# Experts phase: the down router's logits from column tiles of stationary padded weights, with an ACT copy and a folding matmul

## Chip, cores and metric

The kernel runs on one core of one Trainium2 chip. The metric is the device time of one execution in microseconds (us), the median of several runs.

## What is computed

Four blocks are applied to `x` of 16 sequences x 256 tokens x 128 features, each with a residual and a layer norm around it: a state-space block, a mixture of experts, a second state-space block, and six transformer layers. The change is in the mixture of experts, cut here to what matters (`E`=8 experts, `K`=2 kept, `H`=128, `I`=512):

```python
def _moe_linear(x, router_w, expert_w):
    logits = x @ router_w.T
    vals, idx = jax.lax.top_k(logits, K)
    probs = jax.nn.softmax(vals, axis=-1)
    onehot = jax.nn.one_hot(idx, n_exp, dtype=x.dtype)
    combine = jnp.einsum('tk,tke->te', probs, onehot)
    out = jnp.zeros((x.shape[0], expert_w.shape[1]), x.dtype)
    for e in range(n_exp):
        out = out + combine[:, e:e + 1] * (x @ expert_w[e].T)
    return out
xt = x.reshape(b * s, h)
g = _moe_linear(xt, router_gate, w_gate)
u = _moe_linear(xt, router_up, w_up)
inter = jax.nn.silu(g) * u
d = _moe_linear(inter, router_down, w_down)
```

All data is float32. Each float32 matmul of the program stands in the profile as two MATMUL instructions with a weight load each, so counts of rows are twice those in the code.

## The kernel before

`program` runs four phases. `ssm_phase` loads everything that comes later while it computes; `ExpertWeights.fetch` issues the expert weights on SP's queue there. `moe_phase` goes over the 16 sequences in 17 passes; there is no scheduler, each engine runs its own program text and the engines meet at semaphores (`Steps` counts them by name). Pass n does the gate and up routing of sequence n (`R`) and the experts of sequence n-1 (`M`).

In TensorE's program (`run` in the block `tensor`) a pass is, in order: the gate experts into PSUM `pg` (`m_experts(0, ..)`, line 748, with the router logits `r_lg`, line 719, after the first quarter), the up experts into `pu` (`m_experts(1, ..)`), the transposed routing weights (`r_ct`, 728), the transpose of the next sequence (`r_xt`, 709), the down router `m_ld` (line 761), and the down experts of the two token halves into `pdown[0]` = `pg` and `pdown[1]` = `pd` (`m_down(0)`, `m_down(1)`, line 772). `it` is the activated input of the down experts, 4 chunks of 128 features x 256 tokens. In `m_ld` the 128x128 pieces of `it` are stationary and 8 columns of `rd` are streamed.

What turns one pass into the next: ACT copies the transposed routing weights out (`cT`, line 693), SP writes them to DRAM and reads them back broadcast over the partitions (`crow`, `cB`, lines 571 and 575), POOL multiplies the up half into `xcT` (line 586), and DVE, after it has summed the first token half of the down experts (`summed(m, 0)`, line 628), multiplies the gate half (line 655). The next pass of TensorE begins with a wait for that last product (`xg`). DVE also evacuates and evaluates the down router (`lg`, line 648, and `top2`), which must be over before `summed(m, 0)`. ACT takes part in that with one exponential (line 696), ahead of which an activation table is loaded, and then copies the next `xT` (line 678).

The bank `pm[1]` holds three things in turn: the gate and up logits (columns 0 to 31), the down logits (columns 0 to 15), and the transposed routing weights (columns 256 to 511).

Of the kernel before, what the change touches and what calls it, by code (L numbers as in the profile page):

```python
# [20 lines left out]
ALU = mybir.AluOpType  # L21
ACT = mybir.ActivationFunctionType
AX = mybir.AxisListType

NSEQ, L, D, P = 16, 256, 128, 128
# [5 lines left out]
NE, FI = 8, 512  # L31
CF = FI // P
# [12 lines left out]
class Steps:  # L45


    def __init__(self, ctx, nc, name, steps):
        self.sem = ctx.enter_context(nc.semaphore(name))
        self.index, k = {}, 0  # L50
        for s in steps.split():
            s, _, m = s.partition("*")
            k += int(m or 1)
            self.index[s] = k
        self.per = k
# [9 lines left out]
def later(n):  # L65

    return not isinstance(n, int) or n > 0
# [14 lines left out]
def power_rsqrt(eng, st, y, var, half):  # L82

    eng.tensor_tensor(y, var, half, ALU.pow).then_inc(st.sem, 1)
# [30 lines left out]
class ExpertWeights:  # L115
# [3 lines left out]
    def __init__(self, nc, ctx):  # L119
        def sb(name, shape):  # L120
            return ctx.enter_context(nc.sbuf_tensor(name, shape, F32))
        self.wg = sb("b_wg", [P, NE, FI])
        self.wu = sb("b_wu", [P, NE, FI])
        self.wd = sb("b_wd", [P, CF, NE * D])
        self.rgu = sb("b_rgu", [P, 2 * NE])
        self.rd = sb("b_rd", [P, CF, NE])
        self.iota = sb("b_iota", [P, NE])
        self.loaded = ctx.enter_context(nc.semaphore("b_loaded"))

    def fetch(self, e, I):  # L130
        for dst, src in [(self.rgu[:, :], I["b_rgu"]), (self.iota[:, :], I["iota"]), (self.rd[:, :, :], I["b_rd"]),
                         (self.wg[:, :, :], I["b_wg"]), (self.wu[:, :, :], I["b_wu"]), (self.wd[:, :, :], I["b_wd"])]:
            e.dma_start(dst, src).then_inc(self.loaded, 16)


class ScanWeights:
# [22 lines left out]
    def clear(self, e):  # L159
        e.memset(self.am[:, 0, :, :], 0.0).then_inc(self.cleared, 1)  # L160
        e.memset(self.cm[:, :, :], 0.0).then_inc(self.cleared, 1)
        e.memset(self.bw[:, :], 0.0).then_inc(self.cleared, 1)
# [67 lines left out]
def tools(nc):  # L230
    ctx = ExitStack()

    def sb(name, shape, dt=F32):
        return ctx.enter_context(nc.sbuf_tensor(name, shape, dt))

    def ps(name, shape, dt=F32):
        return ctx.enter_context(nc.psum_tensor(name, shape, dt))
    return ctx, sb, ps


def ssm_phase(nc, I, X, ident, experts, scan, layers):


    ctx, sb, ps = tools(nc)
    NP = NSEQ // 2
    with ctx:
# [54 lines left out]
        @block.sync  # L301
        def _(e):
            for dst, src in [(wxd[:, :, :], I["a_wxd"]), (cw[:, :, :], I["a_cw"]), (bias_in[:, :, :], I["a_bias_in"])]:
                e.dma_start(dst, src).then_inc(taps_l, 16)
            e.dma_start(X[:, 0:4, :, :], I["x"][:, 0:4, :, :]).then_inc(xl[0], 16)
            e.dma_start(ind[:, :], I["ind"]).then_inc(loaded, 16)
            e.dma_start(bout[:, :], I["a_bout"].to_broadcast([P, D])).then_inc(bias_l, 16)
            for s in range(4, NSEQ, 4):
                e.dma_start(X[:, s:s + 4, :, :], I["x"][:, s:s + 4, :, :]).then_inc(xl[s // 4], 16)
            experts.fetch(e, I)  # L310
            scan.fetch(e, I)
            layers.fetch(e, I)

        @block.gpsimd
        def _(e):
            for i in range(2):
                e.memset(xpad[i][:, :, 0:TAPS - 1], 0.0).then_inc(gset, 1)
            e.memset(minus[:, :], -0.5).then_inc(gset, 1)
            scan.clear(e)
            e.wait_ge(gset, 3)  # L320
            e.wait_ge(bias_l, 16)
            for s in range(NSEQ):
                e.wait_ge(xl[s // 4], 16)
                e.tensor_tensor(res[:, s, :, :], X[:, s, :, :], bout[:, :].unsqueeze(1).to_broadcast([P, T, D]), ALU.add)\
                    .then_inc(biased, 1)
            for p in range(NP):
                a = 2 * T * p
                e.wait_ge(vn.sem, vn.at("ve", p))
                power_rsqrt(e, gn, y[:, a:a + 2 * T], ve[:, a:a + 2 * T], minus[:, :])
# [178 lines left out]
def moe_phase(nc, I, X, ident, experts):  # L508


    ctx, sb, ps = tools(nc)
    with ctx:
        wg, wu, wd = experts.wg, experts.wu, experts.wd
        rgu, rd, iota = experts.rgu, experts.rd, experts.iota
# [10 lines left out]
        ex = sb("b_ex", [P, 3 * T])  # L525
# [6 lines left out]
        sig = sb("b_sig", [P, CF * L])  # L532
        it = sb("b_it", [P, CF, L])
        acc = sb("b_acc", [P, T, D])
        stats = sb("b_stats", [P, T, 6])
        mv = sb("b_mv", [P, T, 2])
        ve = sb("b_ve", [P, T])
# [6 lines left out]
        pm = [ps("b_pm0", [P, 512]), ps("b_pm1", [P, 512])]  # L544
# [6 lines left out]
        ar = Steps(ctx, nc, "b_act_r", "xT ex ctc")  # L551
        gr = Steps(ctx, nc, "b_pool_r", "xu")
        wide = [ctx.enter_context(nc.semaphore(f"b_wide_{k}")) for k in "gu"]
        pm_ = Steps(ctx, nc, "b_pe_m", "g*2 u*2 ld d0 d1")
        vm = Steps(ctx, nc, "b_dve_m", "gu*2 lc " + route.format(T) + f" acc0*{NE} acc1*{NE} bn*2 ag*2 ve nw*{VRS} out*2")
        am_ = Steps(ctx, nc, "b_act_m", "sig*2 ex")
        block = ctx.enter_context(nc.Block())

        def passes(run, eng):

            for n in range(NSEQ + 1):
                run((n, n % 2) if n < NSEQ else None, (n - 1, (n - 1) % 2) if n else None)
# [26 lines left out]
        @block.vector  # L589
        def _(e):  # L590
            e.wait_ge(loaded, 16 * LOADS)

            def top2(st, act, n, a, b):

# [75 lines left out]
        @block.scalar  # L670
        def _(e):
            def run(R, M):
                if R:
                    n, p = R
                    e.wait_ge(pr_.sem, pr_.at("xt", n))
                    if n >= 2:
                        e.wait_ge(gr.sem, gr.at("xu", n - 2))
                    e.activation(xT[p][:, :], pm[0][:, 0:L], ACT.Copy).then_inc(ar.sem, 1)
                    e.wait_ge(vr.sem, vr.at("df", n))
                    e.activation(ex[:, 0:2 * T], df[:, 0:2 * T], ACT.Exp).then_inc(ar.sem, 1)  # L680
                if M:
                    m, q = M
                    for j in range(2):
                        e.wait_ge(pm_.sem, pm_.at("g", m, 1 - j))
                        if j == 0 and later(m):
                            e.wait_ge(vm.sem, vm.at("gu", m - 1))
                        e.activation(sig[:, j * 512:(j + 1) * 512], pg[:, j * 512:(j + 1) * 512], ACT.Silu).then_inc(am_.sem, 1)
                if R:
                    e.wait_ge(pr_.sem, pr_.at("ct", n))
                    if n:  # L690
                        e.wait_ge(vr.sem, vr.at("xg", n - 1))
                        e.wait_ge(gr.sem, gr.at("xu", n - 1))
                    e.activation(cT[:, :], pm[1][0:2 * NE, L:2 * L], ACT.Copy).then_inc(ar.sem, 1)
                if M:
                    e.wait_ge(vm.sem, vm.at("df", m))
                    e.activation(ex[:, 2 * T:3 * T], df[:, 2 * T:3 * T], ACT.Exp).then_inc(am_.sem, 1)
            passes(run, e)

        @block.tensor
        def _(e):  # L700
            e.wait_ge(loaded, 16 * LOADS)

            def run(R, M):
# [49 lines left out]
                def m_ld():  # L753
                    if M:
                        m, p = M
                        e.wait_ge(vm.sem, vm.at("gu", m))
                        if R:
                            e.wait_ge(ar.sem, ar.at("ctc", R[0]))
                        for t in range(T):
                            for j in range(CF):  # L760
                                last = e.matmul(pm[1][:, t * NE:(t + 1) * NE], it[:, j, t * P:(t + 1) * P], rd[:, j, :],
                                                start=j == 0, stop=j == CF - 1)
                        last.then_inc(pm_.sem, 1)

                def m_down(t):
                    if M:
                        m, p = M
                        if t and later(m):
                            e.wait_ge(vm.sem, vm.at("acc1", m - 1))
                        for b in range(2):  # L770
                            for j in range(CF):
                                last = e.matmul(pdown[t][:, b * 512:(b + 1) * 512], it[:, j, t * P:(t + 1) * P],
                                                wd[:, j, b * 512:(b + 1) * 512], start=j == 0, stop=j == CF - 1)
                        last.then_inc(pm_.sem, 1)
                if R and R[0] == 0:
                    r_xt(0)
# [1131 lines left out]
```

## Time and profile before

| | us |
|---|---|
| median of 3 runs (lowest to highest) | 4251.59 (4249.69 to 4258.62) |
| profiled execution, its own time | 4247.64 |
| span of the profile | 4245.5 |
| TensorE busy | 4079.6 (96%) |
| VectorE (DVE) busy | 3294.3 (78%) |
| ScalarE (ACT) busy | 2414.7 (57%) |
| GpSimd (POOL) busy | 2229.2 (53%) |

The span runs from the first to the last instruction; the execution's own time is 2.1 us longer. The experts phase takes from 76.2 to about 828 us of the span, one pass some 45 us. Busy shares are means over phases with different limits, so what the change is worth has to be read in the experts phase alone, at the places where TensorE waits.

### The profile page before, as it was taken

The page shows a single profiled execution, that of the slowest core. Times are in us where ns is not written, and L with a number is a line of the kernel's source. Part 1 is how long each engine was busy: PE and PEld are TensorE (multiplying, and loading weights), DVE is VectorE, ACT ScalarE, POOL GpSimd, SP SyncE. Part 2 cuts the span into 40 slices and gives each one's busy share as a digit, 9 for nine tenths or more (in the row PEclk, how much of TensorE's full clock was granted, in tenths as well). Part 3 has the DMA queues.
Part 4 walks back from the last instruction along what each step waited for, and adds up shares of the span by engine and source line. Part 5 has one row for each costly group of instructions (what it writes and reads, how often), then busy time and mean ns, then how long its engine had stood idle before and what let it go on. Part 6 is the DMA issues. An engine that isn't in the chain of part 4 may idle for free.

```text
span 4245.5 us, 144543 instructions
## 1 busy us (share of the span) xinstructions
PE 4079.6 (96%) x63655; PEld 2975.9 (70%) x63655; DVE 3294.3 (78%) x6965; ACT 2414.7 (57%) x4394; POOL 2229.2 (53%) x1351
## 2 busy tenths in 40 slices
PE   6999999896999999999999999999999999999997
PEld 4767777673677777777777777777777777776775
DVE  4344444356888888888888888888888888889995
ACT  3010111144667767676676766767767677666664
POOL 2011011025666666666666666666666666666662
PEclk8999999998999999999999999999999999999998
DMA  4111111000111111111111111111111111111110
GB/s 155 40 60 41 40 60 41 20 1 25 37 40 37 51 46 42 41 37 51 46 42 41 37 50 47 42 41 37 51 46 45 38 37 51 46 43 40 45 39 26
DMA packets 76231, 186.16 MB, mean 44 GB/s; under 512 B 15819, under 2 KB 44630, under 8 KB 71126
## 3 DMA queue, kind: packets, MB, share of 16 engines
q1 hardware_dynamic: 74870, 176.51, 13.5%
q8 instruction: 504, 8.26, 0.8%
q14 instruction: 121, 0.99, 0.1%
q10 hardware_dynamic: 736, 0.40, 0.0%
HBM read 61.25 MB, written 2.36 MB: 15 GB/s over the span
## 4 chain that ended last, share of the span: by engine, by line
PE 66%; DVE 5%; ACT 3%; issue 1%; POOL 1%; DMA 0%; DVEq 0%; POOLq 0%; SPq 0%
PE pQ L1666 15%; PE pTO L1699 9%; PE pS L1650 9%; PE pM L1734 7%; PE pTO L1712 7%; PE pM L1723 7%; PE pC L1768 6%; PE pTO L1680 3%; PE pC L1778 3%; ACT sq L1531 2%; ACT pS L1515 1%; DVE rot L1380 1%; DVE m L1384 1%; DVE n L1395 1%; POOL rot L1298 1%
## 5 line engine op out<-in xcount | busy, mean ns | idle before, releaser
L1298 POOL TENSOR_TENSOR rot<-rot,m 128x1024 f32<-128x1024 f32 x384 | 905.4, 2358 | 385.6 <-DVE m L1384 385.6
L1290 POOL TENSOR_TENSOR rot<-rot,rn 128x1024 f32<-128x1024 f32 x384 | 733.0, 1909 | 280.7 <-DVE rn L102 280.7
L1531 ACT ACTIVATE sq<-pQ 128x1024 f32<-128x1024 f32 x380 | 389.5, 1025 | 438.0 <-PE pQ L1666 437.7
L1307 POOL TENSOR_TENSOR E<-E,rc 128x512 f32<-128x512 f32 x384 | 400.7, 1044 | 349.1 <-DVE rc L1370 348.8
L1699 PEld LDWEIGHTS pTO<-PT,V 64*64 64x64 f32 x24576 | 401.8, 134 | 108.5 <-issue 99.8
L1380 DVE TENSOR_TENSOR rot<-pQ,tabl 128x1024 f32<-128x1024 f32 x380 | 456.7, 1202 | 12.1 <-ACT sq L1531 9.9
L1384 DVE TENSOR_TENSOR m<-pQ,tabl 128x1024 f32<-128x1024 f32 x380 | 461.2, 1214 | 0.1
L1650 PEld LDWEIGHTS pS<-kT,qT 64*32 64x32 f32 x24576 | 361.7, 107 | 140.5 <-issue 105.8
L1395 DVE TENSOR_REDUCE n<-sq 128x16 f32<-128x1024 f32 x380 | 459.2, 1208 | 0.0
L1650 PE MATMUL pS<-kT,qT 64*32 64x64 f32 x24576 | 426.6, 218 | 25.1 <-issue 15.5
L1699 PE MATMUL pTO<-PT,V 64*64 64x32 f32 x24576 | 444.2, 221 | 4.0 <-ACT PT L1540 2.5
L1723 PE MATMUL pM<-ident,rot 128*128 128x128 f32 x3072 | 416.7, 279 | 17.8 <-POOL rot L1290 13.2
L586 POOL TENSOR_TENSOR b_xcT<-b_cB,b_xT 128x2048 f32<-128x2048 f32 x16 | 72.2, 4512 | 628.5 <-DMA b_cB<-b_crow 585.9
L1548 ACT ACTIVATE oT<-pTO 128x256 f32<-128x256 f32 x768 | 252.7, 381 | 259.9 <-PE pTO L1699 259.7
L1666 PE MATMUL pQ<-wq,xs 128*128 128x512 f32 x760 | 380.4, 623 | 6.3 <-DVE m L1384 5.6
L1734 PE MATMUL pM<-wv,xs 128*128 128x512 f32 x768 | 362.4, 594 | 3.4 <-ACT XT L1502 3.4
L1723 PEld LDWEIGHTS pM<-ident,rot 128*128 128x128 f32 x3072 | 332.7, 141 | 38.6 <-POOL rot L1290 16.3
L1666 PE MATMUL pQ<-wk,xs 128*128 128x512 f32 x760 | 357.3, 593 | 0.8 <-DVE m L1384 0.8
L1712 PE MATMUL pTO<-oT,wo 128*128 128x256 f32 x1536 | 350.1, 381 | 0.6 <-ACT oT L1548 0.4
L1356 DVE TENSOR_REDUCE mx<-pS 128x8 f32<-128x512 f32 x384 | 262.5, 684 | 70.8 <-PE pS L1650 70.6
L1712 PEld LDWEIGHTS pTO<-oT,wo 128*128 128x128 f32 x1536 | 286.5, 192 | 36.8 <-ACT oT L1548 1.2
L1768 PE MATMUL pC<-xnT,w 128*128 128x256 f32 x1152 | 299.7, 383 | 4.0 <-DVE hh L1436 2.2
(226 smaller groups left out, 6973.9 us busy)
## 6 DMA issues: line engine op xcount, KB each, us to landing
V<-V SPq DMA_DIRECT2D x192, 384.0 KB, 3.5
b_cB<-b_crow SPq DMA_DIRECT2D x32, 1024.0 KB, 6.3
xs<-XT SPq DMA_DIRECT2D x192, 64.0 KB, 2.9
V<-V SPq DMA_DIRECT2D x96, 128.0 KB, 3.3
ys<-XT SPq DMA_DIRECT2D x192, 64.0 KB, 2.2
wq<-in_wqkv SPq DMA_DIRECT2D x6, 512.0 KB, 4.3
wk<-in_wqkv SPq DMA_DIRECT2D x6, 512.0 KB, 4.4
wv<-in_wqkv SPq DMA_DIRECT2D x6, 512.0 KB, 5.6
```

The source lines that it names most:

```text
L1290: e.tensor_tensor(r, r, rn[b % 2][:, c:c + HEADS].unsqueeze(2).to_broadcast([P, HEADS, HD]), ALU.mult)\
L1298: e.tensor_tensor(rot[j % RING][:, :], rot[j % RING][:, :], m2[:, :, :].rearrange("p h d -> p (h d)"), ALU.add)\
L1380: e.tensor_tensor(rot[j % RING][:, :].rearrange("p (h d) -> p h d", d=HD), projected(j)[:, :].rearrange("p (h d) -> p h d", d=HD), tl[:, t ...
L1384: e.tensor_tensor(m2[:, :, :].rearrange("p h (b d) -> p h b d", b=2), projected(j)[:, :].rearrange("p (h b d) -> p h b d", b=2, d=HD // 2) ...
L1395: e.tensor_reduce(n2[:, c:c + HEADS], squared(j).rearrange("p (h d) -> p h d", d=HD), AX.X, ALU.add)\
L1650: x = e.matmul(pS[32 * j:32 * j + 32, b * KEYS:(b + 1) * KEYS], q[r:r + HD, h // 2, WIN * w:WIN * (w + 1)], k[r:r + HD, h // 2, WIN * w:WI ...
L1666: x = e.matmul(projected(j)[:, i * 512:(i + 1) * 512], xs[n % 3][:, t * P:(t + 1) * P], wqkv[w][:, i * 512:(i + 1) * 512], start=True, sto ...
L1699: x = e.matmul(pOV[b % 2][c:c + HD, j // 2, w // 4, WIN * (w % 2):WIN * (w % 2 + 1)], V[n % 2][r:r + KEYS, w // 4, 1 - w % 2, h * HD:(h + ...
L1712: x = e.matmul(pO[:, 0:L], wo[:, c, :], oT[:, c, :], start=c == 0, stop=c == N // P - 1)
L1723: x = e.transpose(pM[i][:, c * P:(c + 1) * P], rot[j % RING][:, (4 * i + c) * P:(4 * i + c + 1) * P], ident[:, :])
L1734: e.matmul(pM[i][:, :], xs[n % 3][:, t * P:(t + 1) * P], wqkv[2][:, i * 512:(i + 1) * 512], start=True, stop=True)\
L1768: x = e.matmul(pC[:, a * L:(a + 1) * L], w1[:, c, :], xnT[:, :], start=True, stop=True)
```

## The change

`m_ld` now keeps the router weights stationary: `rd` is padded with zeros to 32 columns a chunk, the four chunks go to four column tiles of the array (output partitions 32j to 32j+31), and the 256 tokens of `it` stream through each. That gives four partial sums on different partitions. ACT copies them to SBUF (`part`), and a matmul for each token half, with `part` stationary and a matrix `fold` of zeros and ones streamed, adds the four and returns the logits to the old place. These two matmuls (`m_fold`) are issued after the second matmul of `m_down(0)`. `fold` is made once by DVE from the identity. POOL clears `rd` at the start, and SP waits for that before it fetches the expert weights; the load now writes 8 of each 32 columns.

```diff
-        self.rd = sb("b_rd", [P, CF, NE])
+        self.rd = sb("b_rd", [P, CF, 32])
...
+    def clear(self, e):
+        e.memset(self.rd[:, :, :], 0.0).then_inc(self.cleared, 1)
 
     def fetch(self, e, I):
+        e.wait_ge(self.cleared, 1)
...
-... (self.rd[:, :, :], I["b_rd"]),
+... (self.rd[:, :, 0:NE], I["b_rd"]),
...
+            experts.clear(e)
             scan.clear(e)
...
-        pm_ = Steps(ctx, nc, "b_pe_m", "g*2 u*2 ld d0 d1")
+        pm_ = Steps(ctx, nc, "b_pe_m", "g*2 u*2 lp ld d0 d1")
-        am_ = Steps(ctx, nc, "b_act_m", "sig*2 ex")
+        am_ = Steps(ctx, nc, "b_act_m", "sig*2 lp ex")
...
             e.wait_ge(loaded, 16 * LOADS)
+            e.tensor_reduce(fold[:, :], ident[:, :].rearrange("p (j x) -> p x j", j=CF)[:, 0:NE, :], AX.X, ALU.add).then_inc(folded, 1)
...
                     e.activation(cT[:, :], pm[1][0:2 * NE, L:2 * L], ACT.Copy).then_inc(ar.sem, 1)
                 if M:
+                    e.wait_ge(pm_.sem, pm_.at("lp", m))
+                    e.activation(part[:, :], pm[1][:, 0:L], ACT.Copy).then_inc(am_.sem, 1)
                     e.wait_ge(vm.sem, vm.at("df", m))
...
                             e.wait_ge(ar.sem, ar.at("ctc", R[0]))
+                        for j in range(CF):
+                            last = e.matmul(pm[1][32 * j:32 * j + 32, 0:L], rd[:, j, :], it[:, j, :], start=True, stop=True,
+                                            tile_position=(0, 32 * j))
+                        last.then_inc(pm_.sem, 1)
+
+                def m_fold():
+                    if M:
+                        m, p = M
+                        e.wait_ge(am_.sem, am_.at("lp", m))
+                        if m == 0:
+                            e.wait_ge(folded, 1)
                         for t in range(T):
-                            for j in range(CF):
-                                last = e.matmul(pm[1][:, t * NE:(t + 1) * NE], it[:, j, t * P:(t + 1) * P], rd[:, j, :],
-                                                start=j == 0, stop=j == CF - 1)
+                            last = e.matmul(pm[1][:, t * NE:(t + 1) * NE], part[:, t * P:(t + 1) * P], fold[:, :], start=True, stop=True)
                         last.then_inc(pm_.sem, 1)
...
                                                 wd[:, j, b * 512:(b + 1) * 512], start=j == 0, stop=j == CF - 1)
+                                if t == 0 and b == 0 and j == 1:
+                                    m_fold()
```

TensorE's program between the up experts and the next pass, first of before (a row is one instruction of the code; `x7` is seven more alike; the names are tiles of the program, the semaphores waited for in brackets):

```order
L728 MATMUL b_pm<-ident,b_cb 16x128 [waits b_dve_r]
L728 MATMUL b_pm<-ident,b_cb 16x128
L709 MATMUL b_pm<-ident,X 128x128 [waits b_act_r]
L709 MATMUL b_pm<-ident,X 128x128
L761 MATMUL b_pm<-b_rd,b_it 128x8 [waits b_act_r,b_dve_m]
L761 MATMUL b_pm<-b_rd,b_it 128x8 x7
L772 MATMUL b_pg<-b_wd,b_it 128x512 x8
L772 MATMUL b_pd<-b_wd,b_it 128x512 [waits b_dve_m]
```

And the same place of the changed program:

```order
L740 MATMUL b_pm<-ident,b_cb 16x128 [waits b_dve_r]
L740 MATMUL b_pm<-ident,b_cb 16x128
L721 MATMUL b_pm<-ident,X 128x128 [waits b_act_r]
L721 MATMUL b_pm<-ident,X 128x128
L772 MATMUL b_pm<-b_it,b_rd 32x256 [waits b_act_r,b_dve_m]
L772 MATMUL b_pm<-b_it,b_rd 32x256 x3
L793 MATMUL b_pg<-b_wd,b_it 128x512 x2
L783 MATMUL b_pm<-b_fold,b_part 128x8 [waits b_act_m]
L783 MATMUL b_pm<-b_fold,b_part 128x8
L793 MATMUL b_pg<-b_wd,b_it 128x512 x6
L793 MATMUL b_pd<-b_wd,b_it 128x512 [waits b_dve_m]
```

Eight matmuls of 8 columns became four of 256 columns with 32 output rows, and two of 8 columns moved behind two down matmuls, with a wait for ACT.

ACT's program at the end of a pass, of before:

```order
L693 ACTIVATE b_cT<-b_pm 16x256 [waits b_pool_r,b_dve_r,b_pe_r]
L696 ACT_TABLE_LOAD
L696 ACTIVATE b_ex<-b_df 128x2 [waits b_dve_m]
L678 ACTIVATE b_xT<-b_pm 128x256 [waits b_pool_r,b_pe_r]
L680 ACTIVATE b_ex<-b_df 128x4 [waits b_dve_r]
```

And of the changed program:

```order
L703 ACTIVATE b_cT<-b_pm 16x256 [waits b_pool_r,b_dve_r,b_pe_r]
L706 ACTIVATE b_part<-b_pm 128x256 [waits b_pe_m]
L708 ACT_TABLE_LOAD
L708 ACTIVATE b_ex<-b_df 128x2 [waits b_dve_m]
L688 ACTIVATE b_xT<-b_pm 128x256 [waits b_pool_r,b_pe_r]
L690 ACTIVATE b_ex<-b_df 128x4 [waits b_dve_r]
```

The new copy stands between the copy of the routing weights and the table load, which now comes behind it.

## Rows read from the trace of the kernel before

**Rows 1.** Timeline of TensorE in one pass: start us, length us, engine, line, operation, count

```profile
510.81 0.51 PE L719 MATMUL b_pm<-b_rgu,b_xT 128*128 128x16 f32 x4
511.17 10.61 PE L748 MATMUL b_pg<-b_xcT,b_wg 128*128 128x256 f32 x48
521.61 13.98 PE L748 MATMUL b_pu<-b_xcT,b_wu 128*128 128x256 f32 x64
...
536.38 1.95 PE L761 MATMUL b_pm<-b_rd,b_it 128*128 128x8 f32 x16 [0.35 <-DVE b_it L645]
538.18 7.11 PE L772 MATMUL b_pg<-b_wd,b_it 128*128 128x512 f32 x16
...
552.00 3.62 PE L748 MATMUL b_pg<-b_xcT,b_wg 128*128 128x256 f32 x16
```

**Rows 2.** Timeline of the other engines at the end of the same pass

```profile
535.85 0.37 ACT L693 ACTIVATE b_cT<-b_pm 16x256 f32<-16x256 f32 x1 [13.44 <-PE b_pm L728]
536.24 1.28 ACT L696 ACT_TABLE_LOAD   x1
...
538.36 0.17 DVE L648 COPY b_lg<-b_pm 128x16 f32<-128x16 f32 x1 [2.04 <-PE b_pm L761]
...
539.77 0.36 ACT L678 ACTIVATE b_xT<-b_pm 128x256 f32<-128x256 f32 x1
...
545.01 4.52 POOL L586 TENSOR_TENSOR b_xcT<-b_cB,b_xT 128x2048 f32<-128x2048 f32 x1 [41.85 <-DMA b_cB<-b_crow]
545.41 0.35 DVE L628 SCALAR_TENSOR_TENSOR b_acc<-b_pg,b_cb,X 128x128 f32<-128x128 f32 x1 [3.83 <-PE b_pg L772]
...
548.38 3.29 DVE L655 TENSOR_TENSOR b_xcT<-b_cB,b_xT 128x2048 f32<-128x2048 f32 x1
```

**Rows 3.** Timeline, the second turn-over, with a late transfer

```profile
167.75 0.37 ACT L693 ACTIVATE b_cT<-b_pm 16x256 f32<-16x256 f32 x1 [13.44 <-PE b_pm L728]
...
178.62 4.50 POOL L586 TENSOR_TENSOR b_xcT<-b_cB,b_xT 128x2048 f32<-128x2048 f32 x1 [42.02 <-DMA b_cB<-b_crow]
...
185.33 3.72 PE L748 MATMUL b_pg<-b_xcT,b_wg 128*128 128x256 f32 x16 [1.27 <-DVE b_xcT L655]
```

**Rows 4.** Timeline, first and last (15th) turn-over: routing weights copied, POOL's product begins

```profile
123.10 0.37 ACT L693 ACTIVATE b_cT<-b_pm 16x256 f32<-16x256 f32 x1 [13.44 <-PE b_pm L728]
...
132.08 4.52 POOL L586 TENSOR_TENSOR b_xcT<-b_cB,b_xT 128x2048 f32<-128x2048 f32 x1 [35.20 <-DMA b_cB<-b_crow]
...
759.07 0.37 ACT L693 ACTIVATE b_cT<-b_pm 16x256 f32<-16x256 f32 x1 [13.43 <-PE b_pm L728]
...
770.21 4.52 POOL L586 TENSOR_TENSOR b_xcT<-b_cB,b_xT 128x2048 f32<-128x2048 f32 x1 [42.59 <-PE b_pg L772]
...
776.93 14.08 PE L748 MATMUL b_pg<-b_xcT,b_wg 128*128 128x256 f32 x64
```

**Rows 5.** Timeline, the seventh turn-over, with a slow first down group

```profile
397.57 0.37 ACT L693 ACTIVATE b_cT<-b_pm 16x256 f32<-16x256 f32 x1 [13.44 <-PE b_pm L728]
...
399.90 8.81 PE L772 MATMUL b_pg<-b_wd,b_it 128*128 128x512 f32 x16
...
415.42 3.62 PE L748 MATMUL b_pg<-b_xcT,b_wg 128*128 128x256 f32 x16
```

**Rows 6.** Stretches: span, length, busy us (instructions) of PE, PEld, DVE, ACT, POOL, granted clock, DMA, GB/s

```profile
399.87:406.87 7.00, 7.00 (x15) 3.01 (x15) 2.57 (x17) 0.47 (x2) 0.65 (x1) 0.76 0.73 300
```

**Rows 7.** Timeline, TensorE on column tiles: the first phase's, then the transformer's

```profile
42.23 3.68 PE L484 MATMUL a_pu<-a_xpad,a_fused 128*64 128x256 f32 x32 [0.91 <-ACT a_xpad L422]
...
2004.76 1.10 PE L1650 MATMUL pS<-kT,qT 64*32 64x64 f32 x64
2005.78 0.66 PE L1680 MATMUL pTO<-ident,E 128*128 128x128 f32 x4
```

**Rows 8.** Timeline of the start: a memset on POOL, and SP's issue of the router weights

```profile
0.83 0.31 POOL L160 MEMSET c_am<- 128x256 f32 x1
...
6.74 0.65 SPq L133 DMA_DIRECT2D b_rd<-in_b_rd  x1
```

More of the change, by code:

```diff
@@ L125, in __init__ @@
         self.rgu = sb("b_rgu", [P, 2 * NE])
-        self.rd = sb("b_rd", [P, CF, NE])
+        self.rd = sb("b_rd", [P, CF, 32])
         self.iota = sb("b_iota", [P, NE])
         self.loaded = ctx.enter_context(nc.semaphore("b_loaded"))
+        self.cleared = ctx.enter_context(nc.semaphore("b_cleared"))
+    def clear(self, e):
+        e.memset(self.rd[:, :, :], 0.0).then_inc(self.cleared, 1)
     def fetch(self, e, I):
-        for dst, src in [(self.rgu[:, :], I["b_rgu"]), (self.iota[:, :], I["iota"]), (self.rd[:, :, :], I["b_rd"]),
+        e.wait_ge(self.cleared, 1)
+        for dst, src in [(self.rgu[:, :], I["b_rgu"]), (self.iota[:, :], I["iota"]), (self.rd[:, :, 0:NE], I["b_rd"]),
                          (self.wg[:, :, :], I["b_wg"]), (self.wu[:, :, :], I["b_wu"]), (self.wd[:, :, :], I["b_wd"])]:
@@ L534, in moe_phase @@
         acc = sb("b_acc", [P, T, D])
+        part = sb("b_part", [P, L])
+        fold = sb("b_fold", [P, NE])
+        folded = ctx.enter_context(nc.semaphore("b_folded"))
         stats = sb("b_stats", [P, T, 6])
```

## The prediction, made before the changed kernel was run

> **What bounds the kernel now.** I read the timeline of TensorE over one pass of the experts phase first. TensorE goes from group to group without a gap: each group of [rows 1] starts before the one ahead of it has drained, by some 0.16 us (511.17 + 10.61 = 521.78, next start 521.61). The one gap before the pass turns over is 0.35 us ahead of the down router, for DVE's product. So work taken out of TensorE's program here is time, up to the place where something else ends last.
>
> The second view, the other engines at the pass's end [rows 2], shows what that is. After the down experts the next pass needs two products. POOL's waits for a transfer that was set off by ACT's copy of the routing weights, at 535.85, ahead of the down router; it starts 9.16 us later and ends at 549.53. DVE's starts at 548.38, when its sums are done, and ends at 551.67, which is 2.14 us after POOL's end; with no more work than in the passes where POOL is done and it takes about that long, it waits until POOL has finished. So whenever POOL's product is still running, the next pass cannot start before POOL's end plus about 2.2 us. The late turn-over says the same: POOL ends at 183.12, TensorE starts at 185.33 after a wait of 1.27 us [rows 3], 2.21 us later; the last one gives 776.93 - 774.73 = 2.20 [rows 4]. By the Trainium skill (SBUF — State Buffer, the part on the shared DVE and GpSimd port pair) the two engines lock each other out for a whole instruction, and the trace agrees, with 2.14 us from one end to the other.
>
> Count time from ACT's copy. TensorE by itself starts the next pass at 552.00 - 535.85 = 16.15 us [rows 1, 2]. The other chain allows it at (POOL's start) + 4.51 + 2.20 = POOL's start + 6.71. POOL's start after the copy, read in the same way in all 15 turn-overs (first 132.08 - 123.10, last 770.21 - 759.07 [rows 4]): 8.98, 10.87, 9.72, 11.29, 9.00, 10.74, 8.65, 10.28, 9.14, 9.16, 8.77, 8.88, 9.13, 8.69, 11.14. This chain does not pass through the down router, so the change does not shorten it. Slack (9.44 minus the number) is 0.46, none, -, none, 0.44, none, -, none, -, 0.28, 0.67, 0.56, 0.31, 0.75, none. The dashes are turn-overs 3, 7 and 9, where TensorE itself is late: the seventh starts at 415.42 - 397.57 = 17.85 us [rows 5], because the first down group takes 8.81 us instead of 7.11. There the granted clock reads 0.76 over 7 us [rows 6], a stretch of some 3.4 us at 1.2 GHz among full 2.4 GHz. The last turn-over has this too, but its transfer is later still, so it costs nothing.
>
> **The change part by part.** *The old router goes.* From its start to that of the next group are 538.18 - 536.38 = 1.80 us for 16 rows of 0.1125 us [rows 1].
>
> *Column tiles come*: 8 MATMULs of 256 columns. Alone one of that size takes (521.61 - 511.17)/48 = 0.2175 us [rows 1], so with no overlap at all they take 1.74 us. On two column tiles, 32 of that size take 3.68 us, less the last one's 0.38 (0.2175 + 0.16), over 31: 0.1065 each [rows 7], so two tiles run fully beside each other. With outputs of 32 rows, 64 MATMULs of 64 columns take 2005.78 - 2004.76 = 1.02 us, 0.016 each against 0.2175/4 = 0.054 alone [rows 7]: 3.4 at a time. Those, however, use only 64 partitions of input each, and here four different streams of 128 partitions run at once, which no row shows. I take four at a time, 8 x 0.2175/4 = 0.44 us.
>
> What changing over costs: behind a tiled group the next one starts 2004.76 + 1.10 - 2005.78 = 0.08 us before its end, not 0.16 [rows 7]; a little on each side plus the ragged start of the first tile makes it about 0.65 us from the router's start to the next group. The Trainium skill (TensorEngine Tiling (Array Packing), Key Properties) speaks against the change here: switching the tiling mode drains the array. A full drain on both sides would be twice 0.16 us instead of twice 0.08, 0.16 us a pass and some 1.3 us over the phase more than I take; the trace's row has half of that behind a tiled group.
>
> *The fold comes*: 4 MATMULs of 8 columns with full stationary weights. Four of 16 columns set in among the gate experts take 511.17 - 510.81 = 0.36 us; at the old router's rate they take 0.45 [rows 1]. I take 0.40.
>
> So TensorE's part of the pass shrinks by 1.80 - 0.65 - 0.40 = 0.75 us. Bounds: with 0.44 and 0.36, 1.00; with two at a time (0.87 + 0.16), 0.37; with none (1.74 + 0.08) and 0.45, the pass grows by 0.47.
>
> *The wait for ACT.* Behind it in TensorE's queue stands the rest of the down experts, and DVE's sums wait for those. The copy of 128x256 costs ACT 0.36 us, as its `xT` copy [rows 2], and ACT's copy of the routing weights is over before the router starts (536.22 against 536.38). The partials are ready some 0.8 us after the router's start, `part` at about 1.25. The fold is asked for after 0.65 plus four down MATMULs at 7.11/16 = 0.44, 2.4 us. So it is covered with 1.1 us to spare. The table load of 1.28 us stands behind the copy in ACT's order; had it stood ahead, `part` would come at about 1.6 us, still covered. Without the cover the copy would cost about 0.6 us a pass.
>
> *Logits later.* They were out 1.98 us after the router's start (538.36) and will be at about 2.4 + 0.4 + 0.2 = 3.0. DVE's routing then ends 1 us later, while the sums it is needed for start about 0.75 earlier; DVE sat idle 3.83 us just there [rows 2], so 2 us are left. With no overlap of the tiles it is 1 us tighter and still holds. ACT's exponential and its `xT` copy slip by 1 us; that `xT` is used only in the next pass, from 552.00 on.
>
> *Set-up.* The memset of 128x128 costs about half of 0.31 us on POOL, long before SP comes to the router weights at 6.74 us [rows 8]; the first down router comes after 123.10 us [rows 4], so neither SP's wait nor the finer-grained load reaches an engine. `fold` is one small DVE instruction, before the first logits. Nothing.
>
> **The sum.** Per turn-over the gain is 0.75 or the slack, whichever is less: 0.46 + 0.44 + 0.28 + 0.67 + 0.56 + 0.31 + 0.75 = 3.47; the three turn-overs where TensorE itself is late give 0.75 each (seventh: it could start at 8.65 + 6.71 = 15.36), 2.25; the last sequence has no turn-over behind it and gives 0.75. Together 6.5 us, where 16 times 0.75 would be 12. Against the profiled execution, 4247.64 - 6.5 = 4241.1; that execution lies 3.95 us under the median, so for the median I say 4251.6 - 6.5 = 4245.1. What a measurement here can tell from no change is about 0.2%, 8.5 us.
>
> **The rivals.** *The thin stretch no longer lowers the clock (0.25).* The slow down groups come right after a stretch in which TensorE idles briefly and then streams only 8 columns at a time. The change makes that stretch shorter and denser. Then turn-over 3 gains 17.85 - 16.43 = 1.42, the seventh 17.85 - 15.40 = 2.45, the ninth 17.85 - 15.85 = 2.00, the last nothing: 3.6 us more than above, a gain of 10.1, 4241.5. For it: all four drops lie exactly there. Against it: eleven passes with the same stretch keep full clock, and the two halves of the fold are thin again. By the Trainium skill (TensorE: Matmul & The Clock Gate) activity is what keeps the array at full clock, which would speak for this rival; the trace shows the drop in 4 of 15.
>
> *Only two streams at a time (0.12)*: the first phase's row is at exactly two, and it is the only one with 128 partitions of input. The gain a pass is 0.37, the sum 9 x 0.37 + 0.28 + 0.31 = 3.9 us, 4247.7.
>
> *Slower: no overlap at all, the change doesn't do what it says (0.08).* A pass grows by 0.31 to 0.47 us. The four turn-overs that wait for a late transfer with no clock drop absorb it, the other 12 passes pay: 4 to 6 us, 4256. It decides once the router group takes over 1.80 - 0.40 = 1.40 us. Against it, both kinds of column tiles in [rows 7] overlap.
>
> *Clock drops in every pass (0.07)*: TensorE now idles longer for late products. A drop costs 1.70 us where TensorE ends last, less what the other chain absorbs; over the passes that have none now this is some 10 us, and the time 4255. Against it: no drop follows the longest waits directly [rows 3].
>
> **How the numbers follow.** The forecast has 0.43, the rivals 0.25, 0.12, 0.08 and 0.07, and 0.05 stays for what I don't see. Transfers are late by chance: five of 15 were. With none late the forecast would gain 3 us more, with ten late 2 less, and the three runs of before lie 9 us apart. The range 4236 to 4256 takes in the gains of 1.00 a pass and of full clock at its foot and no overlap at its head. Faster by over 0.2% (under 4243.1) is most of the clock rival and a third of the forecast, 0.33; slower by over 0.2% needs two of the losses together, 0.04; the rest, 0.63, is within.
>
> **What the profile will show.** The router group and the next group's start 0.65 us apart (0.44 to 0.6 without any changing over; 1.0 for two streams; 1.8 for none). The fold 0.36 to 0.45 us long, with no wait for ACT. The next pass 15.4 us after the copy of the routing weights where the transfer is early, and POOL's start plus 6.7 where not, with more and longer waits of TensorE for DVE's `xcT`. Transfers 8.7 to 11.3 us as before. Down groups of 8.81 us in none, four, or most passes. The prediction is wrong if the fold waits, if DVE's sums start later than before, or if the turn-overs do not keep to POOL's start.

## The result, and the profile after

The changed kernel takes 4234.79 us (median of 7 runs, 4226.95 to 4236.37) against 4249.69 us (7 runs, 4242.55 to 4258.62): ratio 0.9961, 95% interval 0.9951 to 0.9971. I had forecast a gain of 6.5 us; it is about 15, and the median lies 1.2 us below the foot of my range. Two later measurements of the same kernel give 0.9972 (0.9962 to 0.9983) and 0.9962 (0.9949 to 0.9976). The profiled execution has a span of 4231.2 us, 14.3 less than before.

TensorE at the end of a pass of the changed kernel, the timeline with the columns of [rows 1]:

```profile
526.56 0.64 PE L772 MATMUL b_pm<-b_it,b_rd 128*32 128x256 f32 x8 [0.35 <-DVE b_it L655]
527.13 1.98 PE L793 MATMUL b_pg<-b_wd,b_it 128*128 128x512 f32 x4
528.95 0.51 PE L783 MATMUL b_pm<-b_fold,b_part 128*128 128x8 f32 x4
529.31 5.40 PE L793 MATMUL b_pg<-b_wd,b_it 128*128 128x512 f32 x12
534.55 7.03 PE L793 MATMUL b_pd<-b_wd,b_it 128*128 128x512 f32 x16
542.13 3.07 PE L760 MATMUL b_pg<-b_xcT,b_wg 128*128 128x256 f32 x13 [0.55 <-DVE b_xcT L665]
```

The router group takes 0.57 us to the next start, the fold 0.36, with no wait for ACT. Splitting the down group costs 0.11: 1.82 for four and 5.24 for twelve instructions against 6.95 for sixteen together, from the start at 538.18 [rows 1] to that of the second down group at 545.13. ACT and POOL in the same pass:

```profile
526.03 0.37 ACT L703 ACTIVATE b_cT<-b_pm 16x256 f32<-16x256 f32 x1 [13.43 <-PE b_pm L740]
527.26 0.38 ACT L706 ACTIVATE b_part<-b_pm 128x256 f32<-128x256 f32 x1 [0.86 <-PE b_pm L772]
```

```profile
535.41 4.51 POOL L595 TENSOR_TENSOR b_xcT<-b_cB,b_xT 128x2048 f32<-128x2048 f32 x1 [40.18 <-DMA b_cB<-b_crow]
```

And DVE, the first row of its sums and its product:

```profile
534.83 0.35 DVE L638 SCALAR_TENSOR_TENSOR b_acc<-b_pg,b_cb,X 128x128 f32<-128x128 f32 x1 [2.11 <-PE b_pg L793]
537.80 4.28 DVE L665 TENSOR_TENSOR b_xcT<-b_cB,b_xT 128x2048 f32<-128x2048 f32 x1
```

From the copy of the routing weights to the second down group are 534.55 - 526.03 = 8.52 us; before they were 538.18 + 7.11 - 0.16 - 535.85 = 9.28 [rows 1, 2], so the pass of TensorE is 0.76 shorter. TensorE then waits: POOL ends at 539.92, DVE's product at 542.08, and TensorE starts at 542.13, 2.21 us after POOL's end. The other turn-overs keep to POOL as well: of the 14 that have a copy of the routing weights behind them, 13 take 35.31 or 35.32 us from POOL's start to that copy, and one takes 36.99. The waits of TensorE from 100 to 812 us, with total us, times and longest in us:

```profile
PE b_pg L760 <- DVE b_xcT L665: 9.3, 11, 2.0
PE b_pm L772 <- DVE b_it L655: 6.2, 16, 0.8
```

And the clock: none of the 16 first down groups is slow any more. The one slow stretch of the phase lies behind the longest wait:

```profile
588.27 5.41 PE L760 MATMUL b_pg<-b_xcT,b_wg 128*128 128x256 f32 x16 [2.00 <-DVE b_xcT L665]
```

```profile
588.00:592.00 4.00, 3.73 (x11) 3.03 (x12) 3.61 (x13) 0.00 (x0) 0.00 (x0) 0.64 0.00 0
```

From the span's start to the last second-half down group are 804.49 us, before 814.37: the experts phase gave 9.9 of the 14.3 us by which the two profiles differ.

### The profile page after: what moved, and what is told of

The parts are those of the page before. It is cut to its first block, busy times and chain, and to the rows that moved or that the text cites. A ratio compares the mean times of both kernels' runs of the same rounds, so it can differ in the third digit from the quotient of the medians.

```text
span 4231.2 us, 144433 instructions
## 1 busy us (share of the span) xinstructions
PE 4061.7 (96%) x63591; PEld 2950.2 (70%) x63591; DVE 3306.9 (78%) x6966; ACT 2422.0 (57%) x4410; POOL 2230.0 (53%) x1352
## 4 chain that ended last, share of the span: by engine, by line
PE 66%; DVE 5%; ACT 3%; issue 1%; POOL 1%; DMA 0%; POOLq 0%; DVEq 0%; SPq 0%
PE pQ L1689 15%; PE pTO L1722 9%; PE pS L1673 9%; PE pM L1757 7%; PE pM L1746 7%; PE pTO L1735 7%; PE pC L1791 6%; PE pTO L1703 3%; PE pC L1801 3%; ACT sq L1554 2%; ACT pS L1538 1%; DVE rot L1403 1%; DVE m L1407 1%; DVE n L1418 1%; POOL rot L1321 1%
## 5 line engine op out<-in xcount | busy, mean ns | idle before, releaser
L1403 DVE TENSOR_TENSOR rot<-pQ,tabl 128x1024 f32<-128x1024 f32 x380 | 456.8, 1202 | 12.4 <-ACT sq L1554 10.1
```

Source lines behind the costliest of these rows:

```text
L1403: e.tensor_tensor(rot[j % RING][:, :].rearrange("p (h d) -> p h d", d=HD), projected(j)[:, :].rearrange("p (h d) -> p h d", d=HD), tl[:, t ...
```

## The experiments

"Early" names kernels in which the transpose of the routing weights stands earlier in TensorE's program, so that the transfers no longer decide. "Phase" below is the time from the first turn-over's copy of the routing weights to the 15th's, read from the timelines, and slow groups are counted in these 15 turn-overs.

**The kernel before again.**

> The unchanged kernel once more, for a second profile. Theory A (the clock drops right behind the old router's thin stretch, by chance of phase): three to six of the 15 turn-overs again have a first down group of over 8 us; experts phase, from the first copy of the routing weights to the start of the last second-half down group, 730 us within 4. Theory B (the drops in the first profile were one accident): none or one. On the tail: if the 3.3 us that the first profile of before lost in its last 50 us belong to the kernel, the drop near 4204 us is there again; if they are chance, it is not always. Time 4250 within 5 us, ratio 1.000.

Ratio 0.9996 (0.9987 to 1.0005). Five slow first down groups, in turn-overs 3, 5, 7, 9 and 13; a stretch with one (columns as in [rows 6]):

```profile
308.00:312.00 4.00, 4.00 (x14) 2.23 (x14) 2.28 (x16) 0.74 (x3) 0.00 (x0) 0.64 0.58 242
```

Phase 637.99 us (first profile 635.97). So the slow groups belong to the kernel, four or five of 15. The drop near the end, at some 4206 us, that the first profile had is not there: the program behind the experts' last second-half down group took 3431.1 and 3429.6 us in the two profiles. In all twelve profiles it lies between 3425 and 3437.

**The changed kernel again, twice.**

> The changed kernel once more. Theory A: no drop right behind the router, every turn-over at POOL's start plus 35.3 us to the next copy of the routing weights, at most one drop behind a long wait for a late product; ratio 0.996 to 0.997. Theory B (the gain of the first profile was half luck with transfers and clock): turn-overs bound by TensorE again, ratio 0.998.

> The changed kernel on the same chip as the one above. Theory A: ratio 0.9965, no slow group behind the router in a third profile, all 15 turn-overs at POOL's start plus 35.3 us. Rival (slow groups are as likely as before and were missed twice by luck): two or more.

Ratios 0.9972 and 0.9962, phases 627.18 and 631.73 us (first profile 628.55), no slow first down group in either. That rules out the rival of luck: 0 of 45 turn-overs against 9 of 30. But the third profile has two slow stretches behind long waits for DVE's late product (2.16 and 2.20 us), like the one above. The first of them:

```profile
185.43 5.41 PE L760 MATMUL b_pg<-b_xcT,b_wg 128*128 128x256 f32 x16 [2.16 <-DVE b_xcT L665]
```

**The transpose early, before and changed.**

```diff
-                m_experts(1, 0, 4)
+                m_experts(1, 0, 1)
                 r_ct()
+                m_experts(1, 1, 4)
```

> The kernel before with the transpose of the routing weights moved from behind the up experts to behind their first quarter, so that copy, transfers and POOL's product start some 10 us earlier. Theory A (POOL's and DVE's products lock each other out, and the transfer sets the late turn-overs): no wait of TensorE for the gate product is left after the first; the pass falls to 44.65 us in all 15 turn-overs but those with a clock drop; gain of the four late ones 1.43 + 1.85 + 1.3 + 0.84 = 5.4 us, and a bit more from the last, so ratio about 0.9985. Rival (DVE is late by itself, with its sums): the time stays, ratio 1.000.

> The changed kernel with the same early transpose. Theory A: with the other chain out of the way all 16 passes give the whole 0.87 us, the pass falls to 43.8 us; against the changed kernel the mean turn-over of 44.75 us loses 0.95, 14 us in all: ratio to the kernel before 0.993, and 14 us below the early kernel before. Rival (DVE's product is late anyway, or more waits and drops appear elsewhere): within 4 us of the changed kernel, ratio 0.996.

The early kernel before: ratio 0.9995 (0.9986 to 1.0004). It no longer waits for the gate product, all its waits from 100 to 812 us are these:

```profile
PE b_pm L761 <- DVE b_it L645: 9.5, 16, 0.8
```

Its turn-overs take 44.86 us, not 44.65: the transposes had filled the time until DVE's product, and TensorE now idles 0.57 us ahead of the router instead of 0.35. Four are 46.56, with a slow first down group. So the waits went as expected, and part of the gain was given back. The time itself stayed, as the rival had it; what decides against that rival is that the waits are gone and that the last second-half down group starts at 810.31 us of the profile, 4 to 5 us earlier than in the two profiles of before. The program behind it took 3437.2 us here, the longest of all twelve profiles, and no run says why.

The early changed kernel: ratio 0.9939 (0.9926 to 0.9953), 4223.18 us, the fastest of all. Every turn-over takes 44.09 or 44.10 us and none is slow. Pass against pass without a slow group, 44.86 - 44.09 = 0.77 us: with the transfers out of the way the shorter program is worth its full size every time, and the changed kernel itself was held back by the other chain. The 14 us that I expected it to gain on the changed kernel were some 12 (4223.18 against 4234.98 on the same chip).

**128 columns in the old router.** From the early kernel before, and from the kernel before:

```diff
-        self.rd = sb("b_rd", [P, CF, NE])
+        self.rd = sb("b_rd", [P, CF, P])
...
-                                last = e.matmul(pm[1][:, t * NE:(t + 1) * NE], it[:, j, t * P:(t + 1) * P], rd[:, j, :],
+                                last = e.matmul(pm[1][:, t * P:(t + 1) * P], it[:, j, t * P:(t + 1) * P], rd[:, j, :],
```

> The early kernel before, with the old router's weights padded with zeros to 128 columns: the same 16 MATMULs and weight loads, but 128 columns streamed in each instead of 8, so that the stretch lasts the same 1.8 us and is not thin. Theory A (the clock falls behind the router because so few columns pass through the array there): no or one slow down group instead of four, pass 44.86 us, experts phase 7 us shorter than that of the early kernel before, ratio about 0.998. Rival (it is the length of the stretch with its idle time, or the phase of the pass): three to five slow groups as before, ratio 0.9995.

> The kernel before, transpose where it was, with 128 instead of 8 columns streamed in the old router: the clock part of the change alone. Theory A: no slow group behind the router; TensorE by itself still turns over 16.15 us after the copy, late transfers still cost what they did. The five slow groups of the second profile of before cost 1.70 us each less what late transfers cover, so 4 to 7 us are gained: ratio 0.9985 to 0.999. With the shorter pass on top (0.76 us where there is slack) this should leave the changed kernel 5 to 8 us below it. Rival (the clock part is all of the gain, the shorter pass nothing): ratio 0.997, as the changed kernel.

The router group is hardly longer (529.86 - 527.97 = 1.89 us to the next start, 1.81 in the early kernel before):

```profile
527.97 2.05 PE L767 MATMUL b_pm<-b_rd,b_it 128*128 128x128 f32 x16 [0.57 <-DVE b_it L651]
529.86 1.45 PE L778 MATMUL b_pg<-b_wd,b_it 128*128 128x512 f32 x3
```

but no turn-over is slow. The same stretches of the early kernel before, with a slow group:

```profile
304.00:312.00 8.00, 8.00 (x27) 4.26 (x27) 2.57 (x17) 0.48 (x2) 2.20 (x1) 0.79 0.00 0
```

and of this one:

```profile
304.00:312.00 8.00, 8.00 (x32) 4.41 (x31) 2.57 (x17) 0.48 (x2) 1.68 (x1) 1.00 0.00 0
```

All turn-overs take 44.86 or 44.87 us: the phase falls from 634.89 to 628.12 us, 6.8, which is four times 1.70. The ratio is 0.9971 (0.9961 to 0.9982) against 0.9995. More columns alone, in nearly the same time and with the same idle piece ahead, take the clock drops away; so the length of the group, the idle time ahead of it and the phase of the pass do not bring them about by themselves. By the Trainium skill (TensorE: Matmul & The Clock Gate, the part on what is happening) a gate sets the clock by how busy the array was. These runs agree in kind: ahead of all 13 slow first down groups in the three profiles of kernels with the 8-column router, TensorE ran the same thin group.

With the transpose in its old place the same edit gives 0.9988 (0.9979 to 0.9997), no slow group, phase 632.26 us. So the clock part of the change is about 5 us alone and the changed kernel is some 10 us faster still (4233.92 against 4243.79 on the same chip), more than the 5 to 8 expected. Not all of these 10 us lie in the experts phase: its last second-half down group starts at 810.85 us with the wide router and at 804.49, 803.27 and 807.36 in the three profiles of the changed kernel, 3.5 to 7.6 us earlier. That much the profiles show for the shorter pass; the rest lies behind the phase and is open.

**No overlap of the tiles.**

```diff
-                            last = e.matmul(pm[1][32 * j:32 * j + 32, 0:L], rd[:, j, :], it[:, j, :], start=True, stop=True,
-                                            tile_position=(0, 32 * j))
+                            last = e.matmul(pm[1][0:32, 0:L], rd[:, j, :], it[:, j, :], start=j == 0, stop=j == CF - 1,
+                                            tile_position=(0, 0))
```

> The early changed kernel with all four chunks accumulated on the first column tile, one behind another, and a fold over 32 rows: the tiles' overlap is gone, all else stays. Theory A: router group to next group 1.8 us instead of 0.57, pass 44.09 + 1.2 = 45.3 us, no slow group since 256 columns pass in each; 20 us above the early changed kernel, ratio 0.9985. Rival (the gain is not from the overlap): under 5 us above it, ratio below 0.9955.

```profile
535.61 1.91 PE L772 MATMUL b_pm<-b_it,b_rd 128*32 128x256 f32 x8 [0.57 <-DVE b_it L655]
537.46 1.98 PE L793 MATMUL b_pg<-b_wd,b_it 128*128 128x512 f32 x4
539.37 0.61 PE L783 MATMUL b_pm<-b_fold,b_part 32*128 32x8 f32 x4
539.91 5.42 PE L793 MATMUL b_pg<-b_wd,b_it 128*128 128x512 f32 x12
```

1.85 us to the next start instead of 0.57: the overlap on four column tiles is worth 1.28 us a pass. The fold over 32 rows costs 0.54 instead of 0.36, the four down MATMULs ahead of it take 1.91 instead of 1.82, and the turn-over is 45.66 us, ratio 0.9988 (0.9979 to 0.9997). No slow group. So the pass without the overlap is longer than the 44.86 us of the early kernel before.

**The fold straight behind the router**, early and with the transpose in its old place:

```diff
                 m_ld()
+                m_fold()
                 m_down(0)
...
-                                if t == 0 and b == 0 and j == 1:
-                                    m_fold()
```

> The early changed kernel with the fold straight behind the router group, so that TensorE waits for ACT's copy. Theory A: a wait of 0.5 to 0.7 us a pass, less the 0.1 us that the split of the down group costs now: pass 44.5 to 44.7 us, 7 to 9 us in all, ratio 0.996; with a new idle piece and a thin fold together slow groups may come back, 1.7 us each. Rival (the copy is no more than a semaphore's delay): pass 44.1, ratio 0.994.

> The changed kernel (transpose where it was) with the fold straight behind the router group. Theory A (POOL's start sets the turn-over): of the 0.5 us a pass that TensorE loses, only the part beyond the slack shows; turn-overs at POOL's start plus 35.3 us wherever POOL starts over 9.2 us after the copy, else 44.4 us; with no slow groups 2 to 4 us above the changed kernel, ratio 0.9975; each slow group that comes back adds up to 1.7. Rival (TensorE sets the pass): 8 us above it.

```profile
526.15 0.64 PE L772 MATMUL b_pm<-b_it,b_rd 128*32 128x256 f32 x8 [0.57 <-DVE b_it L655]
527.29 0.61 PE L783 MATMUL b_pm<-b_fold,b_part 128*128 128x8 f32 x4 [0.50 <-ACT b_part L706]
```

Early, TensorE waits 0.50 us for ACT, the turn-over is 44.67 us instead of 44.09, and the ratio 0.9958 (0.9944 to 0.9971) instead of 0.9939: 8 us, what the place of the fold is worth. With the transpose in its old place the same wait is there, and the ratio is 0.9962 (0.9949 to 0.9976), no different from the changed kernel's. That is less than the 2 to 4 us I expected. In 10 of the 14 turn-overs up to the last, POOL's chain covers the wait; they keep to POOL's start plus 35.30 to 35.32 us. In the last pass, behind the 15 turn-overs, a slow first down group is back, with a granted clock of 0.58 from 798 to 802 us:

```profile
797.76 0.61 PE L783 MATMUL b_pm<-b_fold,b_part 128*128 128x8 f32 x4 [0.50 <-ACT b_part L706]
798.23 8.81 PE L793 MATMUL b_pg<-b_wd,b_it 128*128 128x512 f32 x16
```

Here the thin piece is the fold: TensorE idles 0.78 us, runs the router group, idles 0.50 us and runs the fold. It is one group of 32 in the two kernels with the fold in this place, too few to give a rate, but it shows that a first down group can be slow without the old router.

## Why the prediction was wrong

**What bounds the pass: right.** Nothing in the changed kernel contradicts POOL's start plus 6.71 us, and the early kernels show what is left when it is gone: 0.77 us in every pass. Two readings were a little off. A turn-over bound by POOL costs more than the wait: the first gate group then takes 3.72 us instead of 3.62 ([rows 3] and [rows 1]), and to the next copy it is POOL's start plus 35.31 against 44.64 for TensorE by itself. So the slack is 9.33 minus POOL's start and not 9.44, 0.11 less in each of the seven turn-overs that the sum counts by it, and the sum is 5.7 rather than 6.5 us. And six transfers were later than that, not five: the third, at 9.72, is one.

**The size of the TensorE part: right.** Predicted 0.75 us, measured 0.76, a match that owes something to luck: the router group was 0.57 instead of 0.65 and the fold 0.36 instead of 0.40, and the split of the down group costs 0.11, which I had not counted. Behind the router group there is no full drain, the next group starts 0.07 us before its end. Ahead of it TensorE was idle for 0.35 us, so a drain there would not show. The 0.57 us also rule out two streams at a time and no overlap.

**The wait for ACT, the later logits, the set-up: right.** The fold never waits where it stands; DVE was still idle 2.11 us before its sums. Moving the fold shows the 0.58 us a pass that its cover is worth.

**The step that failed is the clock.** The forecast kept the slow down groups, so its sum has nothing for their end; that stood only as the rival "the thin stretch no longer lowers the clock", at 0.25. They ended, in 45 turn-overs of three profiles, at 1.70 us each where TensorE ends last, and the thin stretch of 8 columns was their cause, as the wide routers show: about 5 us alone. I held against it that eleven passes with the same stretch keep full clock; but a cause that acts in four or five of 15 is still a cause, and the thing to weigh was that all four drops lay there and none elsewhere. That rival's own sum, 10.1 us, is close to what the experts phase gave in the first pair of profiles, 9.9, but the closeness is partly luck: it has the 0.11 us too much in its slacks as well, it has no place for the new slow stretch of 1.7 us, and the transfers of the changed kernel's profile were earlier, with POOL's start 9.43 us after the copy on average against 9.63. With the repeats the pairs of profiles range from 7 to 12.

**The rest stays open.** By their ratios the timed runs are 12 to 17 us apart, by the start of the last second-half down group the profiles are 7 to 12 (814.37 and 815.43 against 804.49, 803.27 and 807.36). Behind them, where the two programs are alike, the changed kernel's three profiles take 3426.7, 3429.8 and 3425.5 us and those of before 3431.1 and 3429.6. Five profiles that scatter so do not tell a real 3 us from chance. Over all twelve profiles, the five of kernels that stream the router weights take 3428.6 to 3437.2 us, 3431.0 on average, and the seven of kernels that keep them stationary 3425.3 to 3430.7, 3427.3 on average. That hints at a real difference of some 4 us, though the two groups overlap, and no run was aimed at its cause. The prediction had put everything behind the phase at nothing, and the range was too tight at its foot for that as well.

**Drops for late products: right in kind, small in number.** The rival of more clock drops had TensorE idling longer; a drop came after waits of 2.00, 2.16 and 2.20 us, three times in 45 turn-overs, and cost 1.7 us each. The early changed kernel has none.

## What to carry to other kernels

Before costing a shorter stretch, find the second chain that ends almost as late and write the turn-over as the later of the two: here 12 us of saved TensorE time (16 times 0.76) were worth about half by the sum, until the transfers were set off earlier. Look at what a stretch does to the clock of the work behind it, not only at its own length: if every slow group lies behind the same thin stretch, its price belongs to the stretch, however many passes escape. The better version takes both, the column tiles and the early transpose: ratio 0.9939.

## What the runs showed of the hardware that was not expected

Sixteen MATMULs of 8 columns and sixteen of 128, both with full stationary weights, take 1.81 and 1.89 us, but right behind the first kind the clock fell to 1.2 GHz in 13 of 45 turn-overs (three profiles), behind the second in none of 30. Four column tiles with 128 partitions of different input each ran nearly fully at once: eight MATMULs of 256 columns in 0.57 us to the next group's start, where one alone takes 0.2175 and the same eight on one column tile took 1.85. DVE's product takes 2.28 us where POOL's is over, as in the early changed kernel from 752.90 us on. If it starts while POOL's product runs, it ends some 2.15 us after POOL's end, whether it was begun 1.15 us before that (548.38 [rows 2], end 2.14 us after) or 2.12 us before (537.80 above, end 2.16 us after).
